# VectorE instead of ScalarE applies three layer norms at the end of a two-layer gated attention kernel

## The reference

```python
x = x + tanh(g_xattn[0]) * L0_xattn(layernorm(x), ctx, mask, ...)   # 32 heads of 128
x = x + tanh(g_ffn[0])   * L0_ffn(layernorm(x), 4-bit weights, ...)
x = x + tanh(g_xattn[1]) * L1_xattn(layernorm(x), ctx, ...)         # one head, RMS-normed Q and K
x = x + tanh(g_ffn[1])   * L1_ffn(layernorm(x), ...)                # base product, router, 8 LoRA experts

def layernorm(x, eps=1e-05):
    m = mean(x); v = var(x)          # over the 512 features of a token
    return (x - m) / sqrt(v + eps)
```

## Time and profile before

| | us |
|---|---|
| median of 3 executions (lowest, highest) | 1083.54 (1083.29, 1084.95) |
| profiled execution: span from first to last instruction | 1080.6 |
| TensorE busy (matmuls) | 1015.1 |
| VectorE busy | 563.7 |
| ScalarE busy | 420.2 |
| GpSimd busy | 319.3 |

### The profile page before, as it was taken

How to read it: one execution, slowest core, us unless ns; L and a number is a source line. 1 busy time by engine, 2 the same in 40 slices (tenths; PEclk the granted TensorE clock), 3 DMA queues, 4 the chain that set the end, 5 groups by cost and what they waited for, 6 DMA issues and landing times.

```text
span 1080.6 us, 14894 instructions
## 1 busy us (share of the span) xinstructions
PE 1015.1 (94%) x5200; PEld 853.6 (79%) x5200; DVE 563.7 (52%) x981; ACT 420.2 (39%) x1160; POOL 319.3 (30%) x229
## 2 busy tenths in 40 slices
PE   3999999999999999999999999999999998779978
PEld 3878887888788878887888788878887876658666
DVE  4565605570557055705560656065606579773586
ACT  4454224422452245224522442244225443545520
POOL 2542124212521241225121512151215142343140
PEclk8999999999999999999999999999999998979989
DMA  7111012001200021002010211020100142100002
GB/s 270 40 62 46 19 42 73 35 20 39 78 29 23 35 78 29 26 32 78 29 37 21 78 29 39 19 78 29 39 19 19 32 175 110 40 21 1 1 1 78
DMA packets 15866, 52.62 MB, mean 49 GB/s; under 512 B 2400, under 2 KB 2784, under 8 KB 14944
## 3 DMA queue, kind: packets, MB, share of 16 engines
q1 hardware_dynamic: 15408, 52.21, 14.1%
q10 hardware_dynamic: 432, 0.07, 0.0%
HBM read 50.18 MB, written 2.10 MB: 48 GB/s over the span
## 4 chain that ended last, share of the span: by engine, by line
PE 79%; DVE 12%; issue 5%; ACT 3%; DMA 1%; POOL 0%; DVEq 0%; ACTq 0%; POOLq 0%
PE bank L1085 26%; PE bank L1097 16%; PE bank L1141 16%; PE bank L1195 6%; PE bank L1127 5%; PE bank L1107 5%; PE bank L1118 2%; DVE rinv L733 2%; DVE rinv L722 1%; DVE prob L719 1%; DVE st L788 1%; DVE tt L809 1%; DVE acc L819 1%; ACT kt L533 1%; DMA cols<-in_cols 1%
## 5 line engine op out<-in xcount | busy, mean ns | idle before, releaser
L1085 PE MATMUL bank<-ct,wk 128*128 128x512 f32 x768 | 183.6, 395 | 7.8 <-issue 7.8
L1085 PE MATMUL bank<-xt,wq 128*128 128x512 f32 x768 | 186.0, 393 | 0.0
L1141 PE MATMUL bank<-wvo,ao 128*128 128x512 f32 x768 | 180.5, 392 | 0.0
L1097 PE MATMUL bank<-wvo,ct 128*128 128x512 f32 x768 | 175.9, 389 | 0.0
L1085 PEld LDWEIGHTS bank<-ct,wk 128*128 128x128 f32 x768 | 143.7, 190 | 36.8 <-issue 8.0
L719 DVE TENSOR_TENSOR prob<-bank,bm 128x512 f32<-128x512 f32 x64 | 43.6, 682 | 242.8 <-PE bank L1107 242.8
L1097 PEld LDWEIGHTS bank<-wvo,ct 128*128 128x128 f32 x768 | 144.0, 188 | 29.8
L1085 PEld LDWEIGHTS bank<-xt,wq 128*128 128x128 f32 x768 | 142.4, 188 | 28.7
L1141 PEld LDWEIGHTS bank<-wvo,ao 128*128 128x128 f32 x768 | 142.4, 188 | 28.5
L452 ACT ACTIVATE prob<-prob,nmax 128x128 f32<-128x128 f32 x256 | 99.4, 389 | 91.8 <-DVE nmax L724 91.8
L318 POOL TENSOR_TENSOR wq<-stage,wq 128x512 fp32r<-128x512 f32 x32 | 41.4, 1294 | 287.3 <-ACT wq L436 286.6
(11 more groups left out here) (143 smaller groups left out, 1188.5 us busy)
## 6 DMA issues: line engine op xcount, KB each, us to landing
stage<-in_w SPq DMA_DIRECT2D x64, 512.0 KB, 3.3
craw<-in_ctx SPq DMA_DIRECT2D x4, 512.0 KB, 6.6
xraw<-in_x SPq DMA_DIRECT2D x2, 1024.0 KB, 13.0
bias<-in_bias SPq DMA_DIRECT2D x8, 256.0 KB, 2.7
cs<-in_ctx SPq DMA_DIRECT2D x4, 512.0 KB, 7.8
tmp<-in_x SPq DMA_DIRECT2D x2, 1024.0 KB, 7.8
out<-acc SPq DMA_DIRECT2D x8, 256.0 KB, 2.0
stage<-in_w_key SPq DMA_DIRECT2D x1, 1024.0 KB, 8.4
```

The lines of the kernel that those rows point to most:

```text
L1085: mm = pe.matmul(bank[un[u] % RING][:, :], w[:, i, c, :], t[:, j, c, half(s)], start=(c == 0 and i + j == 0), stop=(c == KC - 1 and i == 1))
L1097: mm = pe.matmul(bank[un[u] % RING][:, :], ct[:, i, c, b * P:(b + 1) * P], wvo[:, j, c, :], start=(c == 0 and i + j == 0), stop=(c == KC - ...
L1141: mm = pe.matmul(bank[un[u] % RING][:, :], ao[:, h, i, b * P:(b + 1) * P], wvo[:, j, h, :], start=(h == heads[0] and i + j == 0), stop=(h ...
```

## The change

For each of the three norms, ScalarE's activation and VectorE's offset go. In their place stands one `tensor_scalar` on VectorE per tile, (acc - mean) x rs1, with both scalars read per partition, the form that the prologue has. For the first two norms it stands where the offset of the half stood (`normed_half`), four tiles one after the other. For the third it stands where the offset of the tile stood (`normed_last`). Nothing is moved in the queues of TensorE, GpSimd and the transfers; the semaphores between offset and activation are gone, and the one that tells of a finished norm is now raised by VectorE. ScalarE's order is otherwise kept; only in the third norm its hi copies, between which the activations stood, now follow one another.

```diff
...
                  "ra", "ra_out", "lg_exp", "router", "hw", "hw_T", "hw_out", "o_mm", "x4", "rows", "rsf", "rsb", "gt", "o_mm2"]
-        names += [f"{n}{i}" for i in range(3) for n in ("bn", "ag", "ve", "rs", "nr", "xn", "T", "hi", "lo")]
+        names += [f"{n}{i}" for i in range(3) for n in ("bn", "ag", "ve", "rs", "xn", "T", "hi", "lo")]
         S = {n: sem(f"t_{n}") for n in names}
...
-                def normed(u, n):
-
-                    act.wait_ge(S[f"nr{n}"], u + 1 if n == 2 else u // HB + 1)
-                    dst, src = tmp[:, u, :], acc[:, u, :]
-                    if n == 0:
-                        dst, src = dst.rearrange("p (s r) -> p r s", s=8), src.rearrange("p (r s) -> p r s", s=8)
-                    act.activation(dst, src, ACT.Identity, bias=nmr[:, u:u + 1],
-                                   scale=rs1[:, u:u + 1]).then_inc(S[f"xn{n}"], 1)
-
                 def weighted(u, t, dst, col, done):
...
                 split_hi(7, "k_T", "k_mm", "k_hi")
-                for u in HALVES[0]:
-                    normed(u, 0)
                 w_split_hi(W_FFN, 2, s_wf, 3)
...
                     split_hi(u, "T0", "k_mm", "hi0")
-                for u in HALVES[1]:
-                    normed(u, 0)
                 for u in range(B):
...
                 for u in HALVES[0]:
-                    normed(u, 1)
-                for u in HALVES[0]:
                     weighted(u, "k_T2", kt1, 2, "k_out")
...
                     weighted(u, "k_T2", kt1, 2, "k_out")
-                for u in HALVES[1]:
-                    normed(u, 1)
...
                 for u in HALVES[0]:
-                    normed(u, 2)
-                    if u:
-                        split_hi2(u - 1)
-                split_hi2(HB - 1)
+                    split_hi2(u)
                 for u in HALVES[0]:
                     ra_out(u)
-                for u in HALVES[1]:
-                    normed(u, 2)
                 router_exp(0)
...
-                def offsets(q, n):
+                def normed(u, n):
+
+                    dst, src = tmp[:, u, :], acc[:, u, :]
+                    if n == 0:
+                        dst, src = dst.rearrange("p (s r) -> p r s", s=8), src.rearrange("p (r s) -> p r s", s=8)
+                    dve.tensor_scalar(dst, src, mv1[:, u, 0:1], rs1[:, u:u + 1],
+                                      ALU.subtract, ALU.mult).then_inc(S[f"xn{n}"], 1)
+
+                def normed_half(q, n):
                     dve.wait_ge(S[f"rs{n}"], q + 1)
-                    dve.scalar_tensor_tensor(out=nmr[:, part(q)], in0=mv1[:, part(q), 0], scalar=-1.0, in1=rs1[:, part(q)],
-                                             op0=ALU.mult, op1=ALU.mult).then_inc(S[f"nr{n}"], 1)
-
-                def offset(u):
+                    for u in HALVES[q]:
+                        normed(u, n)
+
+                def normed_last(u):
                     dve.wait_ge(S["rs2"], u + 1)
-                    dve.scalar_tensor_tensor(out=nmr[:, u:u + 1], in0=mv1[:, u, 0:1], scalar=-1.0, in1=rs1[:, u:u + 1],
-                                             op0=ALU.mult, op1=ALU.mult).then_inc(S["nr2"], 1)
+                    normed(u, 2)
...
                 split_lo(5, "k_hi", "k_lo")
-                offsets(0, 0)
+                normed_half(0, 0)
                 dve.wait_ge(s_early, 80)
...
                 split_lo(3, "hi0", "lo0")
-                offsets(1, 0)
+                normed_half(1, 0)
                 for u in HALVES[1]:
...
                 keys_normed(1)
-                offsets(0, 1)
+                normed_half(0, 1)
                 x2(4)
...
                 split_lo(3, "hi1", "lo1")
-                offsets(1, 1)
+                normed_half(1, 1)
                 for u in HALVES[0]:
...
                         if u % HB:
-                            offset(u - 1)
+                            normed_last(u - 1)
...
                 x3_half(0)
-                offset(HB - 1)
+                normed_last(HB - 1)
                 for u in HALVES[0]:
...
                 x3_half(1)
-                offset(B - 1)
+                normed_last(B - 1)
...
                 dve.tensor_copy(emap[:, :], emap_i[:, :]).then_inc(s_prep, 1)
```

More of the change, by code:

```diff
@@ L153, in build @@
     mv1 = place("mv1", [P, B, 2], fp32)
-    k2ss, k2ms, k2rr, ve1, rs1, nmr, qss, qms, qrr, qsc, nm1, es1, ri1 = (
-        place(n, [P, B], fp32) for n in ("k2ss", "k2ms", "k2rr", "ve1", "rs1", "nmr", "qss", "qms", "qrr", "qsc", "nm1", "es1", "ri1"))
+    k2ss, k2ms, k2rr, ve1, rs1, qss, qms, qrr, qsc, nm1, es1, ri1 = (
+        place(n, [P, B], fp32) for n in ("k2ss", "k2ms", "k2rr", "ve1", "rs1", "qss", "qms", "qrr", "qsc", "nm1", "es1", "ri1"))
     ctx = ExitStack()
```

## The result

The changed kernel took 1087.09 us in the median of 17 executions (1084.29 to 1089.10), the kernel before 1083.56 us in 17 beside it (1082.44 to 1085.23). The ratio is 1.003, with a 95% interval from 1.0022 to 1.0037: 2.4 to 4.0 us slower. The forecast was 1087.7 us, slower with a chance of 0.64.

The account below looks back on a forecast made before the run. TensorE's waits behind VectorE's splits were taken to bound the part changed. 2.9 (to the query product) - 0.9 (second norm's second half) + 2.2 (third norm) = 4.2 us, on 1083.54: 1087.7 us, range 1083.0 to 1091.0.

Parts of the forecast that it names:

- The slack of VectorE: VectorE idles 4.42 us before the key scaling and 4.87 us before 969.14; added work counts only beyond that.
- Plain price: A contiguous norm on VectorE, with no GpSimd work beside it, costs 0.46 us, as in the prologue.
- Beside GpSimd: A VectorE norm while GpSimd adds or subtracts rows costs 1.44 us, one per GpSimd instruction.
- rival C: GpSimd doesn't hold the norms up and strided writing is free, 0.46 us everywhere: -2.7 us, 1080.8 us; chance 0.08.
- D: A norm after 957.39 gets no turn until GpSimd's row is over: +9.0 us, 1092.5 us; chance 0.09.
- The stride: First norm's output, written with a stride of 64 elements, costs VectorE about 0.8 us per norm, from ScalarE's extra 0.37.
- Second norm, first half: From 957.39, VectorE 4.6 us more; with 3.2 from the first norm, less 4.87 idle, 2.9 us late at 969.14.
- Second norm, second half: Before 989.33, ScalarE without norms ends TensorE's 0.94 us wait: minus 0.9 us; VectorE's added 4.5 us cost nothing.
- Third norm: TensorE's restarts at 1023.30 and 1049.64 come 1.1 us later per half: 2.2 us, bounds 1.1 to 3.5.
- The clock: TensorE's half clock behind idle time, 2.8 us around 935, lies beside VectorE's late work and costs nothing.
- Rival A: First norm's strided writing costs VectorE nothing, eight norms at 0.46 instead of 0.8 us: +1.5, 1085.0 us; chance 0.26.
- two signs of being wrong: Prediction is wrong if the query product starts before 969, or if strided norms cost what plain ones do.

Follow-up runs that it names:

- the last kernel: Kernel before, with second norm's late half on VectorE, ScalarE's key weights before norms, base copies after hi copies, GpSimd's additions and query subtractions before roots: 1075.69 us.

## Why the prediction was right, and where it wasn't

The sign and the range held, and the size nearly: 2.4 to 4.0 us slower, where 4.2 were forecast. The mechanism (slack that absorbs work, places that add up) held too, but one of its prices didn't. By steps:

- **The slack of VectorE** (4.42 and 4.87 us) decided, as said. Both idle times went, and only the rest of the added work reached TensorE.
- **Plain price, 0.46 us**: 0.45 from one start to the next (1018.09 to 1018.54). Right.
- **Beside GpSimd, 1.44 us**: 1.41, and the run with GpSimd idle shows its work to be the cause. Right. Rivals C and D, that it doesn't bite or bites for a whole row, fell with it.
- **The stride, 0.8 us: wrong size.** The norms come 0.55 us apart, and 0.46 without the stride. ScalarE's added 0.37 us doesn't carry over to VectorE, which pays about 0.1. On eight norms that is 2.0 us too much, and the shift of the first half came out another 0.4 smaller. So the first norm put VectorE 5.2 us behind, and not 7.6; less the idle time of 4.42 that is 0.6 at the key scaling, counted from the first transposes, and not 3.2. The rule that the prediction named from the Trainium skill, "VectorE: DVE Perf Modes" (What auto-detection actually checks), came nearer to the 0.55 us than the price it took; the penalty of "SBUF — State Buffer" (Door 1, the note on cachelines) is there on VectorE too, but at 0.1 us for 512 elements.
- **Second norm, first half:** 4.5 more on VectorE, where 4.6 were forecast, less 4.87. Right; the query product is 0.1 us late instead of 2.9, through the first norm's error alone.
- **Second norm, second half: 0.9 forecast, 1.5 in the profile.** The wait of 0.94 went; 0.3 came from a product that had less of the half clock, and 0.2 from the next product now overlapping the transposes ahead of it. Alone, it couldn't be told in the time.
- **Third norm, 2.2 us: 2.4 in the profile of the changed kernel**, 1.3 and 1.1 by halves, the added 0.2 being about what the held-up power adds (0.79 us instead of 0.55). By the runs it is more: 2.3 to 5.0 us alone, and the changed kernel against the pair without it, 1.0030 against 0.9997, 3.6 us. The 0.4 to 0.8 us at half clock behind the last restart, which two profiles show, go in that direction. So does the clock of the executions: granted over the whole span it was 0.9775 in the mean of the six with the third norm alone and 0.9808 in the 29 of before beside them, and 0.979 in the 17 of the changed kernel against 0.981 in the twelve of the pair without the third norm. Of 1084 us, 0.001 of full clock is 1.1 us, so by this estimate the clock could be worth up to 2 to 4 us; how much of it fell on products that something waited for is open.
- **The clock** was costed at nothing, as long as it hides behind VectorE. That was too simple. The stretches at half clock came at other times in each kernel, and they gave and took 0.3 to 3 us in single profiles.

So the total was nearer than its parts, and that is luck: 2.9 - 0.9 + 2.2 was forecast, and the profile has 0.1 - 1.5 + 2.4, with 0.8 for the clock, in all 1.9. Two terms erred in opposite directions in the runs: the first norm was priced too high and the third, with what follows it, too low. Rival A, with its free stride and 1.5 us, was in the profile nearer to what happened, but the runs exclude its size. The forecast's own case, a strided norm of 0.6 to 1.0 us, didn't occur: 0.55 lies between it and A. Neither of the prediction's two signs of being wrong occurred either: the query product started at 970.79, and a strided norm cost 0.1 us more than a plain one. One slip changes nothing: rival C's sum counts the third norm at 2.0 us, the forecast at 2.2, and no reason is given.

## What to carry to other kernels

Where two engines have slack at different places, moving an operation is paid at each place apart: count the idle time that it can eat there, and where there is none (a chain of one engine up to the end, as in the third norm here) leave it. Ask of a VectorE `tensor_scalar` from SBUF to SBUF what GpSimd does at that moment; here it was three times the price, and turning GpSimd's queue gave back more than the whole change had cost. And look first at what stands behind a waiting instruction: ScalarE waited 13.45 us before its norms, and the key weights behind them could start as soon as the keys were transposed, 6 us before the norms did in the last kernel. Putting them first was worth more than any norm moved.

## What the runs showed of the hardware

- VectorE's `tensor_scalar` of 128x512 from SBUF to SBUF and GpSimd's `tensor_tensor` of 128x512 take turns: VectorE's operation lasts 1.48 to 1.53 us instead of 0.54, one per GpSimd instruction, and GpSimd's row of four takes longer as well. Not every VectorE operation is held up so: in the changed kernel the statistics (`bn_stats`) of 128x512 took 0.69 us beside the same GpSimd work, at 965.97, as they do elsewhere, and the residual tiles, which read PSUM, 0.74. GpSimd beside the second norm in the changed kernel:

```profile
957.82 5.76 POOL L372 TENSOR_TENSOR acc<-acc,rows 128x512 f32<-128x512 f32 x4
963.55 5.33 POOL L365 TENSOR_TENSOR wt_q<-stage,wt_q 128x512 fp32r<-128x512 f32 x4
```

  5.76 and 5.33 us, against 5.39 and 4.99 in the earlier trace rows. The long wait of 6.10 us didn't recur with any of the norms.
- Writing fp32 with a stride of 64 elements costs VectorE about 0.1 us in 512 elements and ScalarE 0.37, though both write the same tile.
- A small power on GpSimd lasts 0.79 us beside one norm on VectorE and 0.55 alone.
- Stretches of TensorE at half clock lasted between 3.4 and 13.7 us. The last kernel has one wait of 1.83 us before the query product in place of 4.11 and 2.20 us; the clock was at half for 3.4 us there instead of 13.7, the transposes ahead of the product took 2.66 us instead of 4.19, and the product 7.35 instead of 8.52. On the product alone the shorter waits were worth 1.2 us more than their length.
